# Fourier layers of a conv-attention hybrid: mode weights applied after the transposition, the norm applied in the inverse's row copies, and the first step's result stored by mode

## The reference, cut to what matters

```python
xa = x.reshape(B * T, 1, H, W)
xn = _inorm(xa, norm1_w, norm1_b)
k, q, v = three _fno_layer of xn            # 32 heads each
p_attn = softmax(q k^T); av = p_attn v      # over the 32 images of a batch
p = _fno_layer(av, Pcw, Psw, H, W)
a = _inorm(p + xa, attn_w, attn_b)
an = _inorm(a, norm2_w, norm2_b)
m = _fno_layer(an, m0cw, m0sw, H, W, inner_norm=True, act=True)
m = _fno_layer(m, m1cw, m1sw, H, W, inner_norm=True, act=False)
out = _inorm(m, mon_w, mon_b) + a

def _fno_layer(x, conv_w, skip_w, ..., inner_norm, act):
    xf = irfft2(W * rfft2(x)[64 x 33 lowest modes])
    if inner_norm: xf = (xf - mean) / sqrt(var + eps)      # per image
    y = xf + skip_w * x
    return gelu(y) if act else y
```

## Time and profile before

| what | value |
|---|---|
| runs | median 2213.52 us (2212.35 to 2218.34, three runs) |
| the profiled execution | 2215.56 us, its span 2213.8 us |
| busy: PE, DVE, ACT, POOL | 80%, 72%, 50%, 15% of the span |

### The profile page before, as it was taken

How to read it: one execution, slowest core, us unless ns; L and a number is a source line. 1 busy time by engine, 2 the same in 40 slices (tenths; PEclk the granted TensorE clock), 3 DMA queues, 4 the chain that set the end, 5 groups by cost and what they waited for, 6 DMA issues and landing times.

```text
span 2213.8 us, 30514 instructions
## 1 busy us (share of the span) xinstructions
PE 1772.8 (80%) x11462; PEld 1128.2 (51%) x11462; DVE 1586.3 (72%) x2741; ACT 1097.3 (50%) x1636; POOL 333.1 (15%) x424
## 2 busy tenths in 40 slices
PE   8865565599775975706999999999999999975856
PEld 8830111199775975603544444445444554443625
DVE  4379999936835426896888788878886888658545
ACT  4286000023544723354676667776777676775110
POOL 0000000000002004571620053103501121110000
PEclk9886777899897997857999999999999999988988
DMA  6450778300010012200000000000000000030396
GB/s 162 186 138 10 175 162 191 91 1 1 1 40 1 1 40 72 87 3 1 1 1 1 1 1 1 1 1 1 1 1 1 1 1 1 1 114 1 136 323 188
DMA packets 95056, 118.42 MB, mean 53 GB/s; under 512 B 15680, under 2 KB 68288, under 8 KB 94112
## 3 DMA queue, kind: packets, MB, share of 16 engines
q1 hardware_dynamic: 94912, 116.46, 18.5%
HBM read 103.99 MB, written 12.44 MB: 53 GB/s over the span
## 4 chain that ended last, share of the span: by engine, by line
PE 63%; DVE 21%; issue 5%; ACT 4%; DMA 3%; POOL 2%; SPq 1%; POOLq 0%; DVEq 0%; ACTq 0%
DVE U L936 7%; PE PS L412 5%; PE PS L414 5%; PE PS L413 5%; PE PS L431 5%; PE PS L433 4%; PE PS L432 4%; PE PS L1152 4%; PE PS L1119 4%; PE PS L1161 4%; PE PS L394 4%; DVE U L968 3%; PE PS L1262 3%; DMA V<-in_L_ffn_weight 2%; PE PS L1131 2%
## 5 line engine op out<-in xcount | busy, mean ns | idle before, releaser
L781 DVE TENSOR_TENSOR DB<-Z 128x1024 f16<-128x1024 f32 (+2 forms) x288 | 337.0, 1170 | 128.8 <-ACT Z L618 76.5
L615 ACT ACTIVATE Z<-PS,MI 128x1024 f32<-128x1024 f32 (+2 forms) x288 | 300.4, 1043 | 229.7 <-PE PS L414 194.4
L767 DVE TENSOR_REDUCE MI<-PS 128x1 f32<-128x512 f32 (+2 forms) x576 | 359.4, 640 | 53.5 <-PE PS L394 34.0
L618 ACT ACTIVATE Z<-PS,MI 128x1024 f16<-128x1024 f32 (+2 forms) x288 | 298.7, 1037 | 0.0
L936 DVE TENSOR_TENSOR U<-A,U 128x4224 f32<-128x4224 f32 x48 | 215.0, 4551 | 0.0
L1249 PE MATMUL PS<-U 128*32 128x352 f32 x1152 | 131.8, 606 | 91.9 <-DVE U L936 91.9
L583 POOL TENSOR_SCALAR Z<-Z,MI 128x128 f32<-128x128 f32 x128 | 86.1, 683 | 718.8 <-DVE MI L796 718.8
L1249 PEld LDWEIGHTS PS<-U 128*32 128x32 f32 x1152 | 39.6, 131 | 183.0 <-DVE U L936 119.4
L949 POOL TENSOR_TENSOR Z<-Z,A 128x704 f32<-128x704 f32 x2 | 6.0, 2980 | 810.4 <-DVE MI L1692 810.4
L1330 ACT ACTIVATE Z<-PS 128x352 f32<-128x352 f32 x6 | 2.8, 463 | 224.0 <-PE PS L1249 224.0
L431 PE MATMUL PS<-Z,A 128*128 128x512 f16 (+3 forms) x288 | 104.1, 361 | 3.9 <-ACT CST L626 3.6
(11 more groups left out here) (408 smaller groups left out, 3879.1 us busy)
## 6 DMA issues: line engine op xcount, KB each, us to landing
V<-in_L_ffn_weight SPq DMA_DIRECT2D x32, 1024.0 KB, 7.5
U<-e_planes SPq DMA_DIRECT2D x192, 132.0 KB, 5.0
A<-x_planes SPq DMA_DIRECT2D x24, 528.0 KB, 10.3
U<-in_x SPq DMA_DIRECT2D x16, 512.0 KB, 3.7
V<-in_x SPq DMA_DIRECT2D x4, 2048.0 KB, 13.8
Z<-in_x SPq DMA_DIRECT2D x16, 512.0 KB, 4.0
out<-U SPq DMA_DIRECT2D x16, 512.0 KB, 5.0
x_planes<-Z SPq DMA_DIRECT2D x2, 1056.0 KB, 8.0
```

Of the source, the lines that this page charges most:

```text
L615: act.activation(EX32[u % 2][:, 0:w], s, ACT.Exp, scale=SCALE / (QUP * KUP), bias=pb).then_inc(sem("ex_ev"), 1)
L618: act.activation(EHI[u % 3][:, 0:w], s, ACT.Exp, scale=SCALE / (QUP * KUP), bias=pb).then_inc(sem("hi_ev"), 1)
L767: dve.tensor_reduce(bm[:, g % 2, t, k:k + 1], PS[:, 4 + chunk_no[c] % 2, 0:w], AX.X, ALU.max).then_inc(sem("ch_ev"), 1)
L781: dve.tensor_tensor(ELO[u % 3][:, 0:w], EX32[u % 2][:, 0:w], EHI[u % 3][:, 0:w], ALU.subtract).then_inc(sem("lo_ev"), 1)
```

## The change

1. A is laid out [partition, 66, image]; all readers and writers follow. The first step's copies write 264 elements with their neighbours 512 bytes apart; the second step's stationary operands are adjacent columns.
2. In layers 1 and 2 the spectrum goes to PE unweighted. After the transposition partitions are (part, ky) and columns are images, so a mode's weight is a value per partition: ACT (15 groups of two kx) or DVE (2 groups) multiplies with its real part, DVE adds the terms of the imaginary part, two operations per kx, into AM (= A).
3. PE multiplies each kx of the result with itself into one bank (33 matmuls), whose diagonal is an image's sum of squares; DVE takes the diagonal, PE sums it with a matmul with ones, which spreads it over the partitions, and variance, root and reciprocal are made for all images at once.
4. The norm is the scale of the inverse's row copies, four per group, on ACT, and on DVE in 2 of 5 groups (layer 1) or 1 of 5 (layer 2).
5. The weights come by six small DMAs, early, and one row of them is folded on DVE and spread by eight small matmuls ahead of layer 0's inverse.
6. The kept images are made by POOL in one go.
7. Fifteen one-time semaphores become one, counted (`once_dve`).

```diff
+MADE = {"e": 1, "c": 2, "g8": 3, "rc": 4, "rim": 5, "xl": 6, "xs": 7,
+        "xe": 8, "ct": 9, "sd": 10, "p": 11, "pb": 12, "pbt": 13, "mt": 14, "pbar": 15}
-        A = sb("A", [128, N, 2 * KX])
+        A = sb("A", [128, 2 * KX, N])
+        WR = MI[:, 0:4 * KX].rearrange("p (l x c) -> p l x c", l=2, c=2)
+        WN = MI[:, 4 * KX:6 * KX].rearrange("p (l x) -> p l x", l=2)
+        AM = Af.rearrange("p (c x n) -> p c x n", c=2, n=N)
+        BY_DVE = {g for g in range(NTR) if g % 8 == 7}
+            by = lambda l, i: "i1_dve" if i % 5 in ((1, 3) if l == 1 else (2,)) else "i1_sc"
...
@@ SP
+            sp.wait_ge(sem("xg_ready"), 1)
             for i, n in enumerate(("m0cw", "m1cw")):
-                sp.wait_ge(sem("f2_mm_m"), NF2 * (i + 1))
-                sp.dma_start(Af[:, 0:2 * M], io[f"L0_conv_{n}"].rearrange("a b k x c -> (a b) (k x c)")
-                             .broadcast_to([128, 2 * M])).then_inc(sem("mw_in"), 16)
+                for h in range(2):
+                    sp.dma_start(WR[KY * h:KY * h + KY, i].rearrange("p x c -> p (x c)"), ...)
+                sp.dma_start(wrow[:, i], io[f"L0_conv_{n}"][0, :, :, 0, :]).then_inc(sem("mw_in"), 16)
@@ POOL
-            for layer in (1, 2):
-                pool.wait_ge(sem("weights_folded"), layer)
-                real, imag = mode_products(pool, pool_steps.later, slice(MD, M))
...
+            pool.wait_ge(sem("src_ready"), NIM // 2)
+            pool.wait_ge(sem("src_odd"), NIM // 2)
+            for i in range(N):
+                ins = pool.tensor_scalar(U[:, i, :], U[:, i, :], WS[:, 4, i:i + 1], WS[:, 5, i:i + 1], ALU.mult, ALU.add)
+            ins.then_inc(sem("a_kept"), 1)
@@ PE
-                        pe.matmul(o, A[:, :, ky], cst["fwr"], start=True, stop=False)
-                        mm = pe.matmul(o, A[:, :, KX + ky], cst["fwi"], start=False, stop=True)
+                        pe.matmul(o, A[:, ky, :], cst["fwr"], start=True, stop=False)
+                        mm = pe.matmul(o, A[:, KX + ky, :], cst["fwi"], start=False, stop=True)
+            def weighted_modes(layer):
+                pe.wait_ge(sem("z_ready"), layer + 1)
+                def squares(g):
+                    pe.wait_ge(sem("am_ev"), NTR * (layer - 1) + g + 1)
+                    for x in range(2 * g, min(2 * g + 2, KX)):
+                        mm = pe.matmul(PS[:, 4, 0:128], AM[:, 0, x, :], AM[:, 0, x, :] if x else dc_part, start=x == 0, stop=x == KX - 1)
+                    return mm
+                for g in range(NTR):
+                    if g >= 4:
+                        pe.wait_ge(sem("am_ev"), NTR * (layer - 1) + g - 3)
+                    for x in range(2 * g, min(2 * g + 2, KX)):
+                        for c in range(2):
+                            mm = pe.matmul(PS[:, g % 4, 256 * (x % 2) + 128 * c:256 * (x % 2) + 128 * c + 128], Zk[:, c:c + 2, :, x], ident,
+                                           is_transpose=True, start=True, stop=True)
+                    mm.then_inc(sem("tr_mm"), 1)
+                    if g >= 3:
+                        squares(g - 3)
+                for g in range(NTR - 3, NTR):
+                    mm = squares(g)
+                mm.then_inc(sem("once_mm"), 1)
+                pe.wait_ge(sem("dg_ready"), layer)
+                pe.matmul(PS[:, 6, 0:128], ones, image_diag, start=True, stop=True).then_inc(sem("once_mm"), 1)
+            pe.wait_ge(sem("wf_ready"), 1)
+            for i in range(2):
+                for c in range(2):
+                    for h in range(2):
+                        mm = pe.matmul(PS[KY * h:KY * h + KY, 5, 2 * i + c:2 * i + c + 1], wrow[:, i, :, c], ident[0:1, 0:1], start=True, stop=True)
@@ ACT
-                    act.activation(A[:, 4 * k:4 * k + 4, :].rearrange("p n k -> p (n k)"), PS[:, k % 4, 0:264], ACT.Copy)...
+                    act.activation(A[:, :, 4 * k:4 * k + 4].rearrange("p k n -> p n k"), PS[:, k % 4, 0:264].rearrange("p (n k) -> p n k", n=4), ACT.Copy)...
+            def weigh_modes(layer):
+                for g in range(NTR):
+                    if g not in BY_DVE:
+                        act.wait_ge(sem("tr_mm"), layer * NTR + g + 1)
+                        for x in range(2 * g, min(2 * g + 2, KX)):
+                            ins = act.activation(AM[:, :, x, :], PS[:, g % 4, 256 * (x % 2):256 * (x % 2) + 256]..., ACT.Copy, scale=WR[:, layer - 1, x, 0:1])
+                        ins.then_inc(sem("am_act"), 1)
+                        if rows_by(layer, k)[0] == "i1_sc":
+                            for j in range(4):
+                                ins = act.activation(DB[0:66, k % 3, 128 * j:128 * j + 128], PS[0:66, 4 + k % 2, 128 * j:128 * j + 128],
+                                                     ACT.Copy, scale=image_rstd[0:66, 4 * k + j:4 * k + j + 1])
-            keep(slice(0, 24))
@@ DVE
-                dve.tensor_copy(A[:, 4 * k:4 * k + 4, :].rearrange("p n k -> p (n k)"), PS[:, k % 4, 0:264])...
+                dve.tensor_copy(A[:, :, 4 * k:4 * k + 4].rearrange("p k n -> p n k"), PS[:, k % 4, 0:264].rearrange("p (n k) -> p n k", n=4))...
-                real, imag = mode_products(dve, later, slice(0, MD))
...
+                dve.tensor_scalar(Z[:, 2, :], Z[:, 0, :], -1.0, None, ALU.mult).then_inc(sem("z_ready"), 1)
+                for x in range(KX):
+                    t = PS[:, x // 2 % 4, 256 * (x % 2):256 * (x % 2) + 256].rearrange("p (c n) -> p c n", c=2)
+                    if x // 2 in BY_DVE:
+                        dve.wait_ge(sem("tr_mm"), layer * NTR + x // 2 + 1)
+                        later(dve.tensor_scalar(AM[:, :, x, :], t, WR[:, layer - 1, x, 0:1], None, ALU.mult))
+                    else:
+                        dve.wait_ge(sem("am_act"), ...)
+                    first = dve.scalar_tensor_tensor(AM[:, 0, x, :], t[:, 1], WN[:, layer - 1, x:x + 1], AM[:, 0, x, :], ALU.mult, ALU.add)
+                    ins = dve.scalar_tensor_tensor(AM[:, 1, x, :], t[:, 0], WR[:, layer - 1, x, 1:2], AM[:, 1, x, :], ALU.mult, ALU.add)
+                    if x % 2 or x == KX - 1:
+                        ins.then_inc(sem("am_ev"), 1)
+                dve.wait_ge(sem("once_mm"), ONCE[f"gram{layer}"])
+                dve.tensor_tensor(image_diag, PS[:, 4, 0:128], ident, ALU.mult).then_inc(sem("dg_ready"), 1)
+                dve.wait_ge(sem("once_mm"), ONCE[f"var{layer}"])
+                dve.tensor_scalar(image_var, PS[:, 6, 0:128], 2.0 * 128, EPS, ALU.mult, ALU.add).then_inc(sem("var_ready"), 1)
+                dve.wait_ge(sem("root_ready"), 4 + layer)
+                dve.reciprocal(image_rstd, image_var).then_inc(sem("rs_ready"), 1)
+                for k in range(NIM + 1):
+                    if k < NIM and rows_by(layer, k)[0] == "i1_dve":
+                        for j in range(4):
+                            ins = dve.tensor_scalar(DB[0:66, k % 3, 128 * j:128 * j + 128], PS[0:66, 4 + k % 2, 128 * j:128 * j + 128],
+                                                    image_rstd[0:66, 4 * k + j:4 * k + j + 1], None, ALU.mult)
```

More of the change, by code:

```diff
@@ L270, in conv_attn_hybrid, with rows_by @@
         NF2, NTR, NIM = 11, 17, 32
+        BY_DVE = {g for g in range(NTR) if g % 8 == 7}
+        def rows_by(layer, k):
+            by = lambda l, i: "i1_dve" if i % 5 in ((1, 3) if l == 1 else (2,)) else "i1_sc"
+            mine = by(layer, k)
+            return mine, sum(by(l, i) == mine for l in range(1, layer + 1) for i in range(NIM if l < layer else k + 1))
         NU = UB * B
@@ L1146, in inverse, with rows_out @@
                 all_emptied(pe, "tr_ev", layer + 1, NTR)
+            def inverse(layer):
+                if layer:
+                    weighted_modes(layer)
+                else:
+                    plain_modes(layer)
+                def rows_out(k):
+                    if layer:
+                        done, n = rows_by(layer, k)
+                        pe.wait_ge(sem(done), n)
+                    else:
+                        pe.wait_ge(sem("i1_ev"), k + 1)
                 def rows(k):
                     if k >= 2:
-                        pe.wait_ge(sem("i1_ev"), 32 * layer + k - 1)
+                        rows_out(k - 2)
                     for j in range(4):
@@ L1363, in _ @@
                 ins.then_inc(sem("src_odd"), 1)
-            def keep(images):
-                for i in range(images.start, images.stop):
-                    ins = act.activation(U[:, i, :], U[:, i, :], ACT.Identity, scale=WS[:, 4, i:i + 1], bias=WS[:, 5, i:i + 1])
-                ins.then_inc(sem("a_kept"), 1)
-            act.wait_ge(sem("src_ready"), NIM // 2)
-            keep(slice(0, 24))
             for layer in (1, 2):
@@ L1708, in _ @@
-                later(dve.tensor_scalar(lay[:, 2:3], lay[:, 2:3], 2.0, EPS, ALU.mult, ALU.add))
-                dve.scalar_tensor_tensor(lay[:, 2:3], lay[:, 3:4], -1.5, lay[:, 2:3], ALU.mult, ALU.add).then_inc(sem("var_ready"), 1)
-                dve.wait_ge(sem("root_ready"), 4 + layer)
```

(14 more changed lines are left out.)

191 lines of the change are left out of this document (85 added, 106 removed).

## The result

The changed kernel took **2136.4 us** (median of three runs, 2134.2 to 2137.5), the kernel before 2213.5 (2212.4 to 2218.3). The ratio is 0.9645, 95% interval 0.9619 to 0.9670: 3.5% faster. The profiled execution took 2136.4 us, span 2134.5 against 2213.8, so the span is 79.3 us shorter. Predicted were 2137 us and 76.4 us.

What follows compares the result with a forecast made beforehand. PE was taken to bound each forward through slow strided weight loads, and to idle between forward and inverse in layers 1 and 2. Terms summed to -76.4 us: 2139.2 in the profile, 2137 us as median; own range 2126 to 2149, wider 2122 to 2163.

Steps and rivals of the forecast that it cites:

- (a): Second step of the three forwards: adjacent weight columns load faster, net -49.7 us including a slow start in layer 0.
- R2: Rival: weight loads stay slow, by the skill's rule of columns alone or another reason than stride; 2187 us, chance 0.05.
- R3: Rival: layer 0's gain is lost because the work behind its forward waits for something else; 2152 us, chance 0.05.
- (b): Strided copies after the first step: 0.60 us instead of 431 ns, hidden except in layer 1, which has no slack; +5.5 us.
- R4: Rival: strided copies bound all three first steps, slower than before from 1.7 us a copy on; chance 0.03.
- (c): Forward's end to first column step, layers 1 and 2: gap becomes 28.8 us, DVE's products at 0.26 us; -38.3 us.
- (d): Inverse loops of layers 1 and 2: four scaled row copies replace one copy; +1.5 and +1.0 us.
- the half-rate starts: PE restarting at half rate in two inverse loops, behind the gap for root and reciprocal; +2.0 us in all.
- R1: Rival: DVE bounds weighing and loops, operations not overlapping, loops at +4 us each, layer 1's copies +10; 2159 us, chance 0.17.
- (e): Kept images' 128 normalisations move from ACT to GpSimd: no gain, only layer 1's negation on DVE delayed; +0.4 us.
- (f): Weight DMAs hidden; folding a weight row adds eight one-row matmuls on PE's path; +1.2 us.

Runs made afterwards that it cites:

- The layout alone: The kernel before with only A's layout changed, so that the second step's stationary columns are adjacent: 2168.4 us, ratio 0.9791.
- the weighing alone: The changed kernel with the old layout of A and all else as changed: 2183.8 us, ratio 0.9869 against the kernel before.
- the ladder: The kernel before with its mixing matmuls reading 128 stationary columns at sixteen strides: loads 191 ns at stride 1, 312 to 342 from 16 bytes on.
- the bursts: Changed kernel and kernel before, layer 2's first-step copies held until four banks are full: copies start 0.446 us apart strided, 0.340 adjacent.
- the combined version: The changed kernel with DVE's row copies as one tensor_tensor and all 17 product groups weighed with ACT's copies: 2128.2 us, ratio 0.9598.
- the version with 0.8 and 1.7: The changed kernel without the two product groups that DVE does alone, ACT making all 17 groups' scaled copies: 2128.8 us, ratio 0.9602.
- DVE's shorter operation: The changed kernel with DVE's inverse row copies as one broadcast tensor_tensor instead of four tensor_scalar: 2133.2 us, ratio 0.9625.

## Why the prediction was right

The main step held: read the rate of a load and the length of a stall from rows of before, and give both back. That the time came within 1 us of 2137 is luck, though: up to the last norm's matmul the kernel gained 83.6 us instead of 76.4; the later stretch took 4.2 more, at a clock of 0.90 in its last part that no term foresaw; and the forecast took off 2.0 us for the distance of the profiled execution from the median, while after the change the profiled execution is the median.

**(a), the forwards: right in size and cause.** -49.7 predicted; -15.3, -17.2 and -17.2 measured. That includes the cold start: layer 0's forward takes 17.1 us, the others 15.2. The layout alone and the weighing alone show that nothing else did it, and the granted clock was 1.00 in layer 1's forward before and after. A rule of columns alone (R2) is refuted by 341 and 196 ns for the same 128 columns of the same kernel in two layouts, and the ladder gives the reason that L1152 seemed to speak for it: its 66 columns lie 512 bytes apart and take 199 ns, no less than 128 adjacent ones (196), so stride costs there too; PE only isn't held up by it (eight records in 0.92 us). R3 fell too: the copy behind layer 0's forward is 15.6 us earlier, and the end keeps it.

**(b), the strided copies: two readings wrong, both too dear.** The duration was right (0.60 forecast, 0.623 measured), but the sum took the rise of the duration, 0.17 us, where the engine pays the rise of the pitch: 0.106 us, as the bursts show. And "no slack" was wrong. DVE's pairs in layer 1, now bound by DVE itself, follow at 1.91 us:

```profile
583.68 1.10 DVE L1723 TENSOR_SCALAR V<-U,MI 128x128 f32<-128x128 f32 x4
584.68 1.07 DVE L1505 COPY A<-PS 128x264 f32<-128x264 f32 x2
585.59 1.10 DVE L1723 TENSOR_SCALAR V<-U,MI 128x128 f32<-128x128 f32 x4
```

Less two times 0.106 that is 1.70 for DVE before, while the pairs stood at 1.81: that was PE's pace (1.79), which DVE only followed, with 0.11 of slack. The windows agree: of 25 us in this stage DVE was busy for 23.13 before (from 590 us on) and for 24.40 after (from 577 us on). 16 pairs times (1.91 - 1.81) is 1.6 us. Measured are +2.0 in the first profile and +1.4 in the second (573.73 to 607.17, 33.4 us), with the layout alone also +1.4; the granted clock of this stage was 0.91 in the first and 0.93 in the other two. R4 needed copies of 1.7 us; they hold the engine for 0.45.

**(c), the gap: right, and a slip of addition.** The terms as written for it add up to 28.4 us, and the sum put down was 28.8. Measured in layer 1: to the transposes 2.1 us (622.06 to 624.16; forecast 2.2), to the first product 1.7 (to 625.82; forecast 2.2), DVE's products with the two groups of its own 19.5 (to 645.32, where the last of them, begun at 644.98, ends; forecast 17.2 + 2.0 + 0.5 = 19.7), the series behind 4.5 (to 649.79; forecast 4.3). The pitch of 0.26, worked out from ten PSUM copies and the cost of a pointer, is what the rows show. The two groups' 2.0 us is right as well: without them DVE's products took 1.9 to 2.1 us less in three of four gaps, and the gaps shrank by 2.0 and 2.1 in the combined version; the version with 0.8 and 1.7 had a granted clock of 0.87 and 0.93 in its gaps, the combined one 1.00 in both.

**(d) and the half-rate starts: +4.1 against +4.5, but differently made up.** Layer 1 lost 3.1, layer 2 1.0. Layer 1's rows behind the reciprocal do start slowly (16 in 3.42 us), but under the wait for the root, the reciprocal and the first row copy; what remains is the loop's late column steps, 0.27 + 0.18 in five, 2.9 us over 32 steps. R1's bound of DVE thus came at three quarters of its +4 in layer 1 and at a quarter in layer 2, and not at all in the products. How much is ACT's and how much DVE's isn't settled: all rows on ACT is no better, DVE's shorter operation recovers 1.2 of the 3.1, and moving ACT's other work away wasn't tried.

**(e), GpSimd beside DVE: right that PSUM operations don't suffer, wrong about who pays.** GpSimd works from 604.02 to 660.07 (128 operations, 56.05 us), done by 680 as forecast. DVE's products beside it keep their pitch of 0.26. The negation takes 1.27 us beside GpSimd in layer 1 and 1.26 without it in layer 2: no delay. GpSimd pays (its timeline around the negation at 622.83):

```profile
622.03 0.87 POOL L1086 TENSOR_SCALAR U<-U,MI 128x128 f32<-128x128 f32 x2
...
622.89 1.53 POOL L1086 TENSOR_SCALAR U<-U,MI 128x128 f32<-128x128 f32 x1
```

One operation of 0.43 us takes 1.53: it waits out the negation. Four other profiles show the same, 1.46 to 1.53 us. The Trainium skill (SBUF — State Buffer, section Who interferes with whom) calls the shared ports an exclusive lock. Here GpSimd was the one locked out, off the path, so the +0.4 was nothing.

**(f), the fold: half the size.** +0.6 for the mixing with its eight small matmuls, 1.2 forecast; the small weight DMAs cost nothing that a stage shows, as said.

## What to carry to other kernels

Before a float32 stationary operand is laid out, ask whether neighbouring columns share 16 bytes: if they don't, a load is recorded 1.7 times as long (341 against 198 ns), but loads follow each other 2.1 times as slowly, and so the stage bound by them took 2.1 times as long (32.4 against 15.2 us). For an engine that works without pause, PE's weight loads included, use the pitch of an operation in a burst, not its recorded duration, and before you call an engine "without slack", check whether its period is its own or that of the engine it follows. A wait with few large serial steps (a DMA, products over a whole tile, a norm) can be spread over a stage that streams anyway; its new length is the pitch of the slowest engine in the stream, so count its operations first.

## What the hardware showed that was not expected

- Load time against stride, 128 float32 columns: 191 ns at 4 bytes, 197 at 8, 262 at 12, then 312 to 342 from 16 to 512 bytes; from start to start 0.116 us at 4 bytes and 0.243 at 264.
- A copy of 264 elements out of PSUM onto elements 512 bytes apart lasts 623 ns instead of 431 but starts only 0.446 instead of 0.340 us after the one before it.
- A vector operation over 2112 columns (1.27 us) stopped a GpSimd operation for 1.1 us and lost nothing itself (1.27 us beside GpSimd, 1.26 without it).
- The same program's later stages differ by 4 us between executions with equal instructions, all of it in PE's time (1101.6 and 1097.0 us busy) and in the part where the granted clock was 0.90 in one and 0.91 in the other.
